# Attention kernel: head groups share a bank half, and several small steps stand in other slots

## The reference

```python
x = x + 0.5 * ffn(layernorm(x))
x = x + retention(layernorm(x))
x = x + 0.5 * ffn(layernorm(x))
```

```python
q, k, v = (src @ W + b for Wq, Wk, Wv)          # 16 heads of 8 numbers
probs = softmax(q k^T * 8 ** -0.5)
x = layer_norm(src + (probs v) @ Wo + bo)        # "ln1"
keys = x @ router_w + router_b                   # one number per token
expert = floor(keys) mod 4
y = relu(x @ W1[expert] + b1) @ W2[expert] + b2
out = layer_norm(x + y)                          # "ln2"
```

## Time and profile before

| what | value |
|---|---|
| times of 3 runs | 946.7, 948.08, 950.37 us |
| profiled execution | 951.38 us, span 949.3 us |
| TensorE, VectorE, ScalarE, GpSimd busy | 828.5, 762.0, 665.3, 568.6 us |
| first attention stage, first to last maximum | 15.37 to 295.08 us |
| second attention stage, first to last maximum | 563.87 to 838.32 us |
| mean granted TensorE clock | 0.961 of full speed |

### The profile page before, as it was taken

One profiled execution on the slowest core, in us unless ns is written; L12 is line 12 of the kernel. 1 busy time (PEld: TensorE's weight loads), 2 busy tenths in 40 slices (PEclk: granted clock), 3 DMA queues, 4 the chain that ended last, 5 costly groups with the idle time before them and its releaser, 6 DMA issues.

```text
span 949.3 us, 26557 instructions
## 1 busy us (share of the span) xinstructions
PE 828.5 (87%) x8607; PEld 625.8 (66%) x8607; DVE 762.0 (80%) x1935; ACT 665.3 (70%) x1370; POOL 568.6 (60%) x801
## 2 busy tenths in 40 slices
PE   4899899999999688479999979999999999996883
PEld 3566666666666688457877856666666666666883
DVE  5688788888897877669898864888888888978775
ACT  2588788888887477435454554988888888874774
POOL 5135667576665667627777682265765757565666
PEclk9999999999999999889999995999999999998998
DMA  9995698000004667230000000000000000046671
GB/s 288 380 417 82 164 412 362 12 11 22 11 23 134 187 197 236 76 87 2 0 0 0 1 1 2 2 13 12 11 22 11 22 11 11 24 143 201 193 240 48
DMA packets 41812, 96.64 MB, mean 102 GB/s; under 512 B 5224, under 2 KB 25470, under 8 KB 37260
## 3 DMA queue, kind: packets, MB, share of 16 engines
q1 hardware_dynamic: 36236, 83.11, 27.1%
q0 software_dynamic: 5504, 12.63, 3.8%
HBM read 43.64 MB, written 53.13 MB: 102 GB/s over the span
## 4 chain that ended last, share of the span: by engine, by line
PE 45%; DVE 20%; issue 18%; POOL 13%; DVEq 1%; ACT 1%; DMA 1%; POOLq 0%; ACTq 0%
DVE mx L1357 9%; PE duo L576 8%; PE duo L632 7%; PE duo L569 3%; POOL out L1930 3%; DVE qk_lo L1346 2%; PE duo L882 2%; POOL x_mid L1930 2%; PE duo L641 2%; PE duo L861 2%; POOL xs L1922 2%; PE duo L570 2%; PE duo L870 2%; PE duo L723 2%; PE duo L840 2%
## 5 line engine op out<-in xcount | busy, mean ns | idle before, releaser
L1357 DVE TENSOR_REDUCE mx<-duo 128x4 fp32r<-128x1024 f32 x256 | 312.2, 1220 | 73.5 <-PE duo L576 68.4
L1047 ACT ACTIVATE probs<-duo 128x1024 f32<-128x1024 f32 x256 | 263.3, 1029 | 58.3 <-PE duo L582 53.7
L576 PE MATMUL duo<-stacks 32*128 32x256 f32 x1024 | 133.6, 338 | 36.3 <-DVE mx L1357 27.3
L632 PE MATMUL duo<-probs,v_st 128*32 128x256 f32 x2048 | 140.3, 392 | 0.3
L582 PE MATMUL duo<-q_st,stacks 32*128 32x256 f32 x1024 | 131.5, 335 | 0.1
L576 PEld LDWEIGHTS duo<-stacks 32*128 32x128 f32 x1024 | 80.7, 191 | 72.6 <-issue 32.7
L1826 POOL TENSOR_TENSOR a_ln<-mv_ln,eps_ln 128x2 f32<-128x2 f32 x32 | 6.3, 197 | 145.3 <-DVE mv_ln L1322 145.1
L569 PE MATMUL duo<-qk_hi,sel_r 128*128 128x256 f32 x256 | 83.0, 345 | 7.6 <-DVE qk_lo L1346 7.6
L632 PEld LDWEIGHTS duo<-probs,v_st 128*32 128x32 f32 x2048 | 54.1, 110 | 41.5 <-issue 3.4
L723 PE MATMUL duo<-w,xs 128*128 x608 | 77.0, 281 | 4.3 <-DVE hidden L1524 1.8
L582 PEld LDWEIGHTS duo<-q_st,stacks 32*128 32x128 f32 x1024 | 77.9, 188 | 1.4 <-ACT probs L1047 0.5
(11 more groups left out here) (219 smaller groups left out, 2178.8 us busy)
## 6 DMA issues: line engine op xcount, KB each, us to landing
x_sorted<-ret SPq DMA_DIRECT2D x2, 17476.0 KB, 49.0
wbuf<-w_pack SPq DMA_DIRECT2D x38, 512.0 KB
ret<-x_sorted SPq DMA_DIRECT2D x22, 257.0 KB
stacks<-x_sorted SPq DMA_DIRECT2D x12, 257.0 KB
wside<-w_pack SPq DMA_DIRECT2D x38, 66.0 KB
w_pack<-wbuf SPq DMA_DIRECT2D x2, 1024.0 KB, 8.4
decay_rows<-prow SPq DMA_DIRECT2D x1, 1536.0 KB
xs<-x_sorted SPq DMA_DIRECT2D x4, 257.0 KB
```

The costliest lines, as they stand in the source:

```text
L576: return pe.matmul(score_bank[h % 2][:, t * SEQ:(t + 1) * SEQ], q_st[r:r + 32, g, t * P:(t + 1) * P], k_st[r:r + 32, g, :], start=True, st ...
L632: last = pe.matmul(pv_bank[32 * j:32 * j + 32, cols], v_st[:, t, h, :], probs[:, h % RING, t, :], start=(t == 0), stop=(t == TT - 1))
L1047: act.activation(probs[:, h % RING:h % RING + 2, :, :], duo_now[:].rearrange("p (n t q) -> p n t q", n=2, t=TT), ACT.Exp, scale=SCALE).the ...
L1357: dve.tensor_reduce(rows, score_duo[:].rearrange("p (n t k) -> p n t k", n=2, t=TT), AX.X, ALU.max, negate=True).then_inc(max_done, 1)
```

## The change

Four things are changed in the attention stages.

- Packing. `v_st` gets a layout in which the second head group of a half lies 16 columns further, so that `weigh_values` adds both groups into the same 256 columns of the value bank. `out_pv` then copies 256 columns instead of 512, `att_to_tokens` makes four transposes instead of eight, all into bank b, and `normalize` is one reciprocal and one multiplication instead of two of each. The columns of `Wo` and `bv` are permuted on the host to match.
- One copy per expansion. `out_expand` is one ScalarE instruction of 512 columns that adds `ones_col` to queries and keys alike.
- Other slots. `position` goes from slot 4 to 6 and `place` from slots 4 and 5 to 6; `out_v` (the value copy) from slot 0 to 1; `out_hi` (the rounding) from slot 4 to slot 3 on ScalarE, ahead of `shift_q(i, 0)`; the aggregation `layer_norm_moments(i + 2, "prep")` from slot 5 to 4; the early part of the expert table (`early_table`) starts two slots later; `sort_out` is GpSimd's last step in an iteration.
- Moved work. The product of the router key (`route` step 0) is made by GpSimd behind `make_x1`, except for a stage's last batch. GpSimd's normalisation adds a negated mean, which one more small product makes, in place of subtracting the mean.

The diff, cut to what matters here:

```diff
 def weigh_values(b, g):
...
-                wait(pe, un_ready, b * 2)
+                wait(pe, un_ready, b * 2 - 1)
...
-                    pe.wait_ge(un_ready, b * 2 + 1)
-            cols = slice((g % 2) * SEQ, (g % 2 + 1) * SEQ)
+                    wait(pe, un_ready, b * 2)
+            half, second = g // 2, g % 2
+            into = pv_bank[:, half * SEQ:(half + 1) * SEQ]
...
-                    last = pe.matmul(pv_bank[32 * j:32 * j + 32, cols], v_st[:, t, h, :], probs[:, h % RING, t, :],
-                                     start=(t == 0), stop=(t == TT - 1))
+                    first = P * second + VC * j
+                    last = pe.matmul(into[32 * j:32 * j + 32, :], v_st[:, half, t, first:first + VC], probs[:, (g * GH + j) % RING, t, :],
+                                     start=(t == 0 and not second), stop=(t == TT - 1 and second == 1), skip_group_check=True)
...
-        def att_to_tokens(b, t):
+        def att_to_tokens(b):
...
-            o = take("ba"[t], att_ready, b * 2 + t + 1)
-            for g in range(GROUPS):
-                last = pe.transpose(o[:, g * P:(g + 1) * P], att_un[:, g, t * P:(t + 1) * P], ident[:])
+            o = take("b", att_ready, b + 1)
+            for t in range(TT):
+                for half in range(2):
+                    last = pe.transpose(o[:, (2 * t + half) * P:(2 * t + half + 1) * P], att_un[:, half, t * P:(t + 1) * P], ident[:])
...
 TensorE, phase, body:
                     elif p == 4:
                         if live(i, base):
                             expand(i, 3)
                         if live(i - 1, base):
                             weigh_values(i - 1, 2)
-                        if live(i - 3, base):
-                            position(i - 3, base)
...
                     elif p == 6:
+                        if live(i - 3, base):
+                            position(i - 3, base)
                         if live(i + 1, base):
                             expand(i + 1, 0)
                         if live(i - 1, base):
-                            att_to_tokens(i - 1, 0)
-                            att_to_tokens(i - 1, 1)
+                            att_to_tokens(i - 1)
...
 def out_expand(b, g):
-            act.activation(q_st[:, g, :], o[:, 0:SEQ], ACT.Copy).then_inc(ex_ready, 1)
-            act.activation(k_st[:, g, :], o[:, SEQ:2 * SEQ], ACT.Identity, bias=ones_col[:]).then_inc(ex_ready, 1)
+            act.activation(both_st[:, :, g, :], o.rearrange("p (n t) -> p n t", n=2), ACT.Identity, bias=ones_col[:]).then_inc(ex_ready, 1)
...
 def out_pv(b, half):
-            act.activation(att_un[:, 2 * half:2 * half + 2, :], pv_bank[:].rearrange("p (a q) -> p a q", a=2),
-                           ACT.Copy).then_inc(un_ready, 1)
+            act.activation(att_un[:, half, :], pv_bank[:, half * SEQ:(half + 1) * SEQ], ACT.Copy).then_inc(un_ready, 1)
...
 ScalarE, phase, body:
                     if p == 0 and live(i, base):
                         out_expand(i, 1)
-                        out_v(i)
...
+                    if p == 1 and live(i, base):
+                        out_v(i)
...
+                    if p == 3 and live(i + 1, base):
+                        out_hi(i + 1)
                     if p == 3 and live(i, base):
                         shift_q(i, 0)
...
-                    if p == 4 and live(i + 1, base):
-                        out_hi(i + 1)
                     if p == 4 and live(i, base):
                         out_expand(i, 3)
...
 def normalize(b):
+            m = bank_b[:].rearrange("p (n c) -> p n c", c=VC // 2)
+            dve.reciprocal(rsum[:], m[:, :, HD]).then_inc(rsum_ready, 1)
+            dve.wait_ge(rsum_ready, b + 1)
+            dve.tensor_tensor(att.rearrange("p t (n d) -> p (t n) d", d=HD), m[:, :, 0:HD],
+                              rsum[:].unsqueeze(2).to_broadcast([P, TT * NH, HD]), ALU.mult).then_inc(att_ready, 1)
...
 VectorE, phase, body:
                     if p == 0:
                         if live(i - 3, base):
-                            for n in range(3):
+                            for n in range(0 if is_last(i - 3, base) else 1, 3):
                                 route(i - 3, base, n)
...
-                            place(i - 3, base, 0)
+                        if live(i + 2, base) and not ahead(i, base):
+                            layer_norm_moments(i + 2, "prep")
                     elif p == 5:
                         if live(i + 1, base):
                             split_qk(i + 1)
+                    elif p == 6:
                         if live(i - 3, base):
-                            place(i - 3, base, 1)
-                            place(i - 3, base, 2)
-                        if live(i + 2, base) and not ahead(i, base):
-                            layer_norm_moments(i + 2, "prep")
-                    elif p == 6:
-                        if live(i - 1, base):
-                            normalize(i - 1, 0)
+                            for n in range(3):
+                                place(i - 3, base, n)
...
                         if live(i - 1, base):
-                            normalize(i - 1, 1)
+                            normalize(i - 1)
...
 def rstd(b, which, steps=1):                          # GpSimd
+            if steps == 1:
+                pool.tensor_tensor(s["c"][:], s["mv"][:, :, 0], minus_one[:], ALU.mult).then_inc(neg_mean[which], 1)
...
-                pool.tensor_scalar(dst(t), src(t), s["mv"][:, t, 0:1], s["rstd"][:, t:t + 1], ALU.subtract, ALU.mult).then_inc(done, 1)
+                pool.tensor_scalar(dst(t), src(t), s["c"][:, t:t + 1], s["rstd"][:, t:t + 1], ALU.add, ALU.mult).then_inc(done, 1)
...
                     make_x1(i - 2, base)
+                    route_product(i - 2, base)
                     own_row(i - 2, base)
...
-                if live(i - 3, base):
-                    sort_out(i - 3, base)
                 if live(i + 2, base):
                     rstd(i + 2, "prep")
...
                     add_bo(i + 2, base)
+                if live(i - 3, base):
+                    sort_out(i - 3, base)
```

78 lines of the change are left out of this document (44 added, 34 removed).

## The result

The changed kernel takes 954.84 us (median of 20 runs, 950.49 to 966.72), the kernel before 949.56 us (20 runs, 940.56 to 955.15): a ratio of 1.0073 with a 95% interval of 1.0043 to 1.0104. It is slower, by 4 to 10 us. The profiled executions differ less: 953.85 against 951.38 us, spans 952.0 and 949.3.

The account below looks back on a forecast made before the run. Bound by a chain through eight slots (burst, VectorE maximum, next burst; 1.93 us a link). Loop +10.8, written-out iterations +7.8, iteration 4 -4.8, start and drain -0.2: +13.6 on 948.08, predicted 962 us, range 950 to 979.

Parts of the forecast that it names:

- half covered stall: Rival, slot 4: the expansion could come earlier, leaving 0.55 us of stall per iteration and an even loop; 947 us, chance 0.12.
- 3 and 19: Written-out iterations 3 and 19: the same net loss as in the loop, +1.1 us together.
- 14 and 30: Written-out iterations 14 and 30: the stall, less table steps that leave slot 5; +0.8 us.
- The step on the rounding: ScalarE, slot 3: the rounding's wait for the fourth expansion delays slot 4's exponential and slot 5's burst, +1.09 us per iteration.
- The lower bound: Slot 5's burst: the least the stall could cost, with every hop at 0.05, was +0.93 us per iteration.
- One marker: VectorE: the maxima of slots 4 and 5 would stand 3.1 us apart instead of 2.0.
- the rest of the loop: Slots 1 and 6: gains of 0.26 and 0.29 us against the 1.09 stall, net +0.54 per iteration, +10.8 over 20.
- The written-out iterations: Ten iterations outside the loops (0 to 3 and 14 of each stage) with the same stall; with iteration 16, +7.8 us.
- The step on iteration 4: GpSimd: sorting last no longer delays batch 5 by its wait for the clearing DMA; iteration 4 gives back 4.77 us.
- the clock did not fall in the loop: Rival: TensorE's stalls lower its clock to the 1.2 GHz level for a third of the time; about 1015 us, chance 0.10.
- Everything else gives back more: Rival, slots 0, 3, 5, 6, 7: other gains exceed the stall; 932 to 946, say 937 us, chance 0.10.
- The Trainium skill's rule: Work on the busiest engine: VectorE's relief of 0.41 us shortens some 28 iterations; about 932 us, within the faster case's 0.10.

Follow-up runs that it names:

- e1_hi4: The changed kernel with the rounding (out_hi) back in slot 4, behind that slot's exponential; 947.09 us, ratio 0.9912 to the kernel before.
- e2_hi3: The kernel before with only the rounding moved to slot 3, ahead of shift_q(i, 0) and slot 4's exponential; 998.84 us, ratio 1.0496.
- e3_mid: The changed kernel with the rounding still in slot 3 but behind shift_q(i, 0); 962.14 us, ratio 1.0095 to the kernel before.
- i4_after_sort: The changed kernel with the sorting back ahead of the next batch's preparation on GpSimd, rounding left in slot 3; 955.59 us, ratio 1.0021.
- e4_sort: The kernel before with only sort_out moved behind the next batch's preparation on GpSimd; 956.38 us, ratio 1.0035.
- i1_hi3_sort: The kernel before with the rounding in slot 3 and the sorting behind the next batch's preparation; 979.30 us, ratio 1.0262.
- i2_route: g_place with the router product back on VectorE; 933.67 us, ratio 0.9821 to the kernel before.
- i3_eight: g_place with eight transposes in slot 6 instead of four, each made twice; 934.88 us, ratio 0.9850 to the kernel before.
- g_place: The changed kernel with the rounding back in slot 4 and the sorting back ahead of the next batch's preparation; 928.47 us, ratio 0.9765.
- g_direct: Meant to make the second loop's transfers plain, but the edit never took effect: e1_hi4's instructions again, on another chip; 928.28 us, one run.
- g_beat7: e1_hi4 with six more one-element GpSimd operations ahead of the sorting's two indirect transfers; 939.94 us, ratio 0.9855 to the kernel before.

## Why the prediction was right, and where it was not

It said 962 with a range of 950 to 979 and slower; measured 954.84. The direction and the cause held. The size did not: the medians differ by 5.3 us, not by 13.6, and 954.84 lies halfway between the forecast and the 947 of the half covered stall. That the range holds it is owed to its width; only the traces tell the two apart. The terms of the sum, by the two profiled executions (what the iterations lost, in us):

| term | forecast | measured |
|---|---|---|
| 19 loop iterations without iteration 4 | +10.3 | +5.6 |
| iteration 4 | -4.2 | -4.4 |
| 3 and 19 | +1.1 | +0.1 |
| 2 and 18 | +1.9 | +1.5 |
| 14 and 30 | +0.8 | -1.2 |
| 0, 1 and 17 | +2.1 | +2.3 |
| 16 | +1.9 | -0.8 |
| start, the part between the stages, the end | -0.2 | -0.4 |
| sum | +13.6 | +2.6 |

The step on the rounding held in every hop: wait ended by the expansion, exponential 2.21 us behind its burst instead of 0.59, one TensorE gap of 1.21 us ended by `probs`, +1.06 to +1.09 us per iteration. (The lower bound was summed wrongly: with every hop at 0.05 it is 239.07 + 0.71 + 0.26 + 1.03 + 0.05 - 240.14 = 0.98, not 0.93.) e1_hi4, e2_hi3, e3_mid and i4_after_sort confirm it from four sides. One marker was wrong for it: the maxima of slots 4 and 5 are 2.92 us apart and not 3.1, because the maximum of slot 4 now starts 1.01 us behind its burst and not 0.83; the burst itself comes earlier by slot 3's 0.11, and VectorE has one more wait ahead of this maximum, for the statistics of batch i + 2. In e2_hi3, which moves the rounding alone, it is 0.82 still, and the maxima are 3.10 apart as forecast. The place to measure a wait of TensorE is the burst.

The step that failed is the rest of the loop: "Loop: +1.09 - 0.26 - 0.29 = +0.54". Slot 6 gave the 0.28. Slot 1 gave 0.35, because the hop from the maximum to the next burst fell from 0.24 to 0.16 with it. Slots 3 and 7 gave 0.11 and 0.09 that I had counted at nothing; both are hops between the maximum's end and the next burst (0.24 to 0.13 and 0.25 to 0.16), and no run isolates their cause. The runs exclude some: the two hops are long in e2_hi3, e4_sort and i1_hi3_sort and short in i2_route and i3_eight, so it is not the rounding's place, the sorting's, the product or the number of transposes. With 0.10 lost in slot 0 of the first loop the net is +0.29, not +0.54, per iteration.

The written-out iterations were worth +1.9 and not +7.8. In 14 and 30 the stall came (slot 4 by maxima 2.11 to 3.20), but slot 5, which some table steps left, fell from 2.86 to 1.93; I had credited these steps with some 0.3 in all. No run isolates them. In 3 and 19 slot 0 fell from 2.33 and 2.40 to 1.83. In 16 I priced the moved rounding at +1.9; the iteration fell by 0.8, beside the clock that rose from 0.61 to 0.81 on average over the iteration. How much of it belongs to the clock is not shown.

The step on iteration 4 had the right size and a wrong cause, so its success was in part luck. It read the 3.40 us of the earlier trace rows as the wait for the clearing DMA, which the sorting's new place would hide. Rows of the kernel before that I did not use say otherwise. The clearing, by the list of DMA issues for the first 100 us (bytes, us to landing), and its issue in the timeline of SyncE:

```profile
x_sorted<-ret SPq DMA_DIRECT2D x1, 17476.0 KB, 49.0
```

```profile
26.48 1.06 SPq L449 DMA_DIRECT2D x_sorted<-ret  x1
```

It landed at 26.48 + 49.0 = 75.5, 17 us ahead of the issue. Two ticks of GpSimd stand around the wait on it, the second behind it, and one row has both, back to back:

```profile
88.74 0.33 POOL L1862 TENSOR_TENSOR tick<-ones_wide 1x1 f32<-1x1 f32 x2
```

So the wait on the clearing had ended by 89.07, and the issue began at 92.47. The changed kernel, and two kernels with the sorting ahead of the preparation, g_place and i4_after_sort:

```profile
93.37 0.33 POOL L1885 TENSOR_TENSOR tick<-ones_wide 1x1 f32<-1x1 f32 x2
93.89 1.22 POOL L1902 DMA_INDIRECT x_sorted<-rows,pos_all  x1 [0.19 <-issue]
```

```profile
87.94 0.33 POOL L1885 TENSOR_TENSOR tick<-ones_wide 1x1 f32<-1x1 f32 x2
88.45 1.22 POOL L1902 DMA_INDIRECT x_sorted<-rows,pos_all  x1 [0.19 <-issue]
```

```profile
93.53 0.33 POOL L1885 TENSOR_TENSOR tick<-ones_wide 1x1 f32<-1x1 f32 x2
94.05 1.22 POOL L1902 DMA_INDIRECT x_sorted<-rows,pos_all  x1 [0.19 <-issue]
```

In g_place the issue follows at 88.45, 4 us earlier than it did before, with 0.19 us of idle time. So it was not the clearing, and with the changed GpSimd program the sorting's place does not matter. In the kernel before and in e2_hi3, the two with this wait (3.40 and 3.51 us), the trace has an 8 KB packet of an instruction queue inside it (at 90.5 and 93.8 us). In e4_sort and i1_hi3_sort, where the order of GpSimd's steps alone is changed, that packet comes 1.6 to 1.8 us ahead of the ticks and nothing waits; in the kernels with the changed GpSimd program it comes at other times. GpSimd waiting for its own code would fit; the trace does not say whose code the packet carries and no run takes it away, so it is not shown, and the cause stays open.

The rivals: the stall was not half covered, and the clock did not fall in the loop (1.00 in both stages; 28 times 2 us more than 962 would be 1018, not 1015). "Everything else gives back more" was wrong for the change as it stands, but its size was nearer than I thought: without the stall an iteration takes 16.33 us (g_direct and g_place), 0.58 less than before. The Trainium skill's rule (Perfetto Trace Analysis, Identifying the Most-Contended Engine) asks for VectorE's relief; the iteration of g_place is 0.58 shorter, of which i2_route gives the product 0.07 in sum and 0.20 to 0.27 in its slot, so the trace agrees with the direction and not with its 0.41.

That the medians differ by 5.3 us and by the ratio's interval 4 to 10, while the profiled executions differ by 2.5, stays partly open: the profile is one execution each, and the experiments show that executions of one program differ by up to 1.2 us per iteration in one slot.

The loops of the second stage, iterations 20 to 29, of the kernel before, the changed one, e1_hi4's profiled run and g_place, in this order, show the sum of it all. The columns are those of the earlier trace rows:

```profile
core 0: us, PE busy (x) PEld busy (x) DVE busy (x) ACT busy (x) POOL busy (x), PEclk, DMA share, GB/s
637.67:806.86 169.19, 157.32 (x1840) 109.16 (x1839) 147.30 (x340) 144.52 (x270) 109.86 (x170) 1.00 0.04 16
```

```profile
638.46:810.36 171.90, 153.22 (x1801) 105.91 (x1800) 142.91 (x311) 140.24 (x230) 104.13 (x202) 1.00 0.04 16
```

```profile
624.82:796.52 171.70, 155.62 (x1801) 105.82 (x1800) 149.93 (x311) 141.95 (x230) 104.22 (x202) 1.00 0.04 16
```

```profile
622.81:786.18 163.37, 153.73 (x1801) 105.63 (x1800) 146.51 (x310) 141.42 (x230) 103.92 (x201) 1.00 0.05 16
```

TensorE has 4 us less work in ten iterations and needed 2.7 us longer; with the rounding back and the sorting ahead it needs 5.8 us less.

## What to carry to other kernels

A copy that waits for another engine's late work must not stand ahead of the backbone's instruction in the same in-order queue: the cost is the wait's end plus everything queued behind it, and both could be added up from rows to a few hundredths. Find the wait's end in the releasing engine's row, and measure the result where that engine is waited for, not at a step with a wait of its own. When one engine is relieved at another's cost, look whether the other's chain is waited for in the faster kernel too: GpSimd sat idle for 5.62 us ahead of its chain in the changed kernel and was waited for in g_place. And before a wait is given a cause, look for a marker instruction that stands behind the wait: it says whether the wait had ended.

## What the runs showed of the hardware that I had not expected

In three kernels, beside GpSimd's second indirect issue (0.96 us, 0.30 us behind the first of 1.11), releases by TensorE reached VectorE and ScalarE up to 1.25 us late, although both were idle: in e1_hi4 in slot 2, in e2_hi3 in slot 0, in e3_mid in slot 2. The late instructions start between 0.4 us ahead of the issue's end and 0.9 us behind it. Another execution of the very same program, on another chip, had none of it. Whether the release was late or the matmuls behind it, the trace doesn't tell, as their ends are modelled. The Trainium skill (SBUF — State Buffer, Who interferes with whom) says that VectorE and GpSimd share a pair of ports and that TensorE and ScalarE have their own. VectorE's small operations agree: 0.45 instead of 0.15 us beside an issue in g_beat7. The late exponentials on ScalarE do not follow from it. The cause is open.

The profiled execution of g_place, with the two issues between 0.12 and 2.49 us behind the burst of slot 0, showed none of these delays.
